# Causal masks of a temporal attention: from mask matmuls to a fused add-and-maximum and a zeroing of the exponentials

## The reference

```python
def _temporal_experts(xt, idx, ...):
    ...
    logits = jnp.einsum('bthd,bshd->bhts', q, k) * HD ** (-0.5)
    causal = jnp.tril(jnp.ones((T, T), dtype=bool))
    logits = jnp.where(causal, logits, -jnp.inf)
    att = jax.nn.softmax(logits, axis=-1)
    o = jnp.einsum('bhts,bshd->bthd', att, v).reshape(B, T, D)
...
xn = _ln(x, norm_s_w, norm_s_b)
spatial_out = _spatial_experts(xn, idx_s, ...)      # attention S, no mask
xt = _ln(x, norm_t_w, norm_t_b)
temporal_out = _temporal_experts(xt, idx_t, ...)    # attention T, causal
fused = _cross_mha(spatial_out, temporal_out, ...)  # attention C, no mask
x = x + fused
```

## The kernel before, in words

| slot | projected, for the next slot | scored | logits from n = 8 | last 8 logits, for n < 8 |
|---|---|---|---|---|
| S slot | T of i | S of i | C of i-2 | T of i-1 |
| T slot | C of i-1 | T of i | S of i | C of i-2 |
| C slot | S of i+1 | C of i-1 | T of i | S of i |

## Time and profile before

### The profile page before, as it was taken

One profiled execution on the slowest core, in us unless ns is written; L12 is line 12 of the kernel. 1 busy time (PEld: TensorE's weight loads), 2 busy tenths in 40 slices (PEclk: granted clock), 3 DMA queues, 4 the chain that ended last, 5 costly groups with the idle time before them and its releaser, 6 DMA issues. The chain is left out here.

```text
span 1797.6 us, 37140 instructions
## 1 busy us (share of the span) xinstructions
PE 1598.6 (89%) x9686; PEld 738.5 (41%) x9686; DVE 1274.2 (71%) x3085; ACT 1217.8 (68%) x2393; POOL 697.2 (39%) x673
## 2 busy tenths in 40 slices
PE   4659946889999999999999999999999999955998
PEld 1217932334444444434444344444444443211665
DVE  5986856388787877878787787878787787352442
ACT  3325741757888878788878878787887878714333
POOL 7822441234344344344334334434434433221442
PEclk9768955989999999999999999999999999857999
DMA  2211125354565455465456456446545635030122
GB/s 51 74 43 37 47 47 71 43 80 60 65 77 66 64 71 79 54 75 74 57 70 77 67 61 79 62 60 76 70 63 69 81 52 65 2 36 26 57 61 59
DMA packets 131811, 108.99 MB, mean 61 GB/s; under 512 B 21809, under 2 KB 124721, under 8 KB 131761
## 3 DMA queue, kind: packets, MB, share of 16 engines
q1 hardware_dynamic: 129712, 104.18, 41.5%
q0 software_dynamic: 2048, 4.20, 0.9%
HBM read 20.05 MB, written 8.39 MB: 16 GB/s over the span
## 5 line engine op out<-in xcount | busy, mean ns | idle before, releaser
L1000 ACT ACTIVATE probs<-psum 128x512 f32<-128x512 f32 (+3 forms) x1536 | 739.6, 551 | 262.4 <-PE psum L1111 159.7
L888 DVE TENSOR_REDUCE mx_S<-psum 128x1 f32<-128x512 f32 x512 | 323.1, 682 | 77.0 <-PE psum L1096 76.5
L888 DVE TENSOR_REDUCE mx_C<-psum 128x1 f32<-128x512 f32 x512 | 319.0, 682 | 56.8 <-PE psum L1096 55.2
L888 DVE TENSOR_REDUCE mx_T<-psum 128x1 f32<-128x128 f32 (+3 forms) x512 | 240.4, 488 | 120.7 <-PE psum L1099 109.5
L824 POOL TENSOR_TENSOR rem_q<-f_q,parts_q 128x512 f32<-128x512 f32 x48 | 55.5, 1155 | 496.9 <-ACT parts_q L986 480.0
L1096 PE MATMUL psum<-ks_S,qs_S 96*128 96x512 bf16 x512 | 201.7, 400 | 26.4 <-DMA ks_S<-parts_k 21.8
L1096 PE MATMUL psum<-ks_C,qs_C 96*128 96x512 bf16 x512 | 202.7, 397 | 12.5 <-DMA ks_C<-parts_k 7.4
L1111 PE MATMUL psum<-qs_C,ks_C 99*128 99x512 bf16 x512 | 194.7, 392 | 18.0 <-ACT probs L1000 10.7
L1111 PE MATMUL psum<-qs_S,ks_S 99*128 99x512 bf16 x512 | 196.0, 384 | 1.6 <-ACT probs L1000 0.9
L1096 PE MATMUL psum<-ks_T,qs_T 96*128 96x128 bf16 (+3 forms) x512 | 157.5, 310 | 7.1 <-DMA ks_T<-parts_k 6.0
L1111 PE MATMUL psum<-qs_T,ks_T 99*128 99x256 bf16 (+3 forms) x512 | 153.3, 302 | 2.5 <-ACT probs L1000 1.7
(11 more groups left out here) (184 smaller groups left out, 2732.5 us busy)
## 6 DMA issues: line engine op xcount, KB each, us to landing
qs_S<-parts_q SPq DMA_DIRECT2D x96, 128.0 KB, 4.5
ks_S<-parts_k SPq DMA_DIRECT2D x96, 128.0 KB, 7.0
qs_T<-parts_q SPq DMA_DIRECT2D x96, 128.0 KB, 4.4
ks_T<-parts_k SPq DMA_DIRECT2D x96, 128.0 KB, 7.0
qs_C<-parts_q SPq DMA_DIRECT2D x96, 128.0 KB, 4.5
ks_C<-parts_k SPq DMA_DIRECT2D x96, 128.0 KB, 6.9
w_in_S<-in_s_in SPq DMA_DIRECT2D x16, 257.0 KB, 2.7
w_in_T<-in_t_in SPq DMA_DIRECT2D x16, 257.0 KB, 2.7
```

The lines of the kernel that those rows point to most:

```text
L888: nc.vector.tensor_reduce(mx[kind][:, n:n + 1], psum[:, ring_place(kind, b, n, RL), 0:last_key], AX_X, ALU.max)\
L1000: nc.scalar.activation(probs[:, n // 4 % 2, n % 4, t0:T], psum[:, LOGITS + ring_place(kind, b, n, RC), t0:T], ACT.Exp, scale=SCALE).then_i ...
```

## The change

- No mask matmul is left, and the tiles `ident_bf`, `mask_row` and `mask_col` go. Scores and logits of T keep their widths; the future half of the diagonal blocks now holds unmasked values.
- `reduce` of T: VectorE's `tensor_tensor_reduce` adds a tile `causal` (128x512, zeros, with -1e30 in the future half of its last 128 columns) to the scores and takes the maximum of the sum in the same instruction; the sum itself is written to a tile `masked`. An increment of a semaphore that nobody waits for (`scored_seen`) stands in front.
- `cut_future`: once the four tiles of a `weigh` are exponentiated, GpSimd's `affine_select` writes zeros into the future half of the four diagonal blocks of `probs2`. `weigh` of T waits for `cut` in place of `exped`.
- GpSimd's sequence is rewritten around the cuts: `split` becomes `remainder` and `low_part`, and the `affine` of `xt` moves from the C slot to the end of the T slot.
- VectorE's start of `attend` waits for `causal`.

```diff
+                def cut_future(kind, b, q):
+
+                    if kind != "T" or not exists(b):
+                        return
+                    pool.wait_ge(exped, TILES * unit_no("T", b) + 4 * q + 4)
+                    pool.sem_inc(cut_seen, 1)
+                    t0 = first_key("T", 4 * q)
+                    diagonal = probs[:, q % 2, :, t0:t0 + P]
+                    nc.gpsimd.affine_select(out=diagonal, in_=diagonal, compare_op=ALU.is_ge, fill=0.0, base=0,
+                                            pattern=[[0, 4], [1, P]], channel_multiplier=-1).then_inc(cut, 1)
...
-                    (kn, bn), _, _, (ko, bo) = units(i, slot)
-                    split(kn, bn)
+                    (kn, bn), _, (kb, bb), (ko, bo) = units(i, slot)
+                    cut_future(ko, bo, 5)
+                    cut_future(ko, bo, 6)
+                    remainder(kn, bn, 0)
+                    cut_future(ko, bo, 7)
+                    remainder(kn, bn, 1)
+                    low_part(kn, bn, 0)
+                    cut_future(kb, bb, 0)
+                    low_part(kn, bn, 1)
                     if exists(bo):
                         u = unit_no(ko, bo)
                         pool.wait_ge(high_out, u + 1)
                         pool.wait_ge(low_out, u + 1)
                         nc.gpsimd.tensor_tensor(s_all[:], s_all[:], s_high[:], ALU.add).then_inc(s_merged, 1)
                         nc.gpsimd.tensor_tensor(u_all[:], u_all[:], u_high[:], ALU.add).then_inc(u_merged, 1)
+                    cut_future(kb, bb, 1)
...
+                    cut_future(kb, bb, 2)
...
                         nc.gpsimd.tensor_tensor(oT[:], u_all[:], s_recip[:], ALU.mult).then_inc(o_ready, 1)
+                    cut_future(kb, bb, 3)
+                    cut_future(kb, bb, 4)
                     if slot == 1 and exists(i + 1):
                         pool.wait_ge(desk_full, desk_use("vS", i) + 1)
                         affine(xn, i + 1, 0, "xn")
-                    if slot == 2 and exists(i + 1):
                         pool.wait_ge(desk_full, desk_use("vT", i) + 1)
                         affine(xt, i + 1, 1, "xt")
...
-                    last_key = P * (n % NB + 1) if kind == "T" else T
-                    nc.vector.tensor_reduce(mx[kind][:, n:n + 1], psum[:, ring_place(kind, b, n, RL), 0:last_key], AX_X, ALU.max)\
-                        .then_inc(reduced, 1)
+                    tile = psum[:, ring_place(kind, b, n, RL), :]
+                    if kind == "T":
+                        dve.sem_inc(scored_seen, 1)
+                        last_key = P * (n % NB + 1)
+                        nc.vector.tensor_tensor_reduce(masked[:, n % RL, 0:last_key], tile[:, 0:last_key],
+                                                       causal[:, T - last_key:T], 1.0, NEG, ALU.add, ALU.max,
+                                                       mx[kind][:, n:n + 1]).then_inc(reduced, 1)
...
-                    pe.wait_ge(exped, TILES * u + 4 * q + 4)
+                    if kind == "T":
+                        pe.wait_ge(cut, 2 * NB * b + q + 1)
+                    else:
+                        pe.wait_ge(exped, TILES * u + 4 * q + 4)
```

More of the change, by code:

```diff
@@ L696, in attend @@
         exped = sem("exped2")
+        cut = sem("cut")
+        cut_seen, scored_seen = sem("cut_seen"), sem("scored_seen")
         summed = sem("summed2")
@@ L814, in affine, with remainder @@
                     nc.gpsimd.tensor_tensor(to[:], scaled[:], s, ALU.add).then_inc(affine_done, 1)
-                def split(kind, b):
+                def remainder(kind, b, c):
                     if not exists(b):
                         return
[L820 to L829, removed]
@@ L831, in slot_program, with low_part @@
-                def slot_program(i, slot):
-                    (kn, bn), _, _, (ko, bo) = units(i, slot)
-                    split(kn, bn)
+                    n = 2 * unit_no(kind, b) + c
+                    pool.wait_ge(hi_done, n + 1)
+                    at_least(pool, mid_done, n - 1)
+                    nc.gpsimd.tensor_tensor(rem[c][:], f32[c][:], parts[c][:, 0, :], ALU.subtract)\
+                        .then_inc(rem_done, 1)
+                def low_part(kind, b, c):
+                    if not exists(b):
+                        return
+                    pool.wait_ge(mid_done, 2 * unit_no(kind, b) + c + 1)
+                    nc.gpsimd.tensor_tensor(parts[c][:, 2, :], rem[c][:], parts[c][:, 1, :], ALU.subtract)\
+                        .then_inc(lo_done, 1)
@@ L862, in _ @@
                 affine(xn, 0, 0, "xn")
-                nc.gpsimd.memset(mask_row[:], 0.0)
-                nc.gpsimd.memset(mask_col[:], 0.0)
+                nc.gpsimd.memset(causal[:], 0.0)
                 for k in KINDS:
@@ L867, in _ @@
                 last.then_inc(ones_in, 1)
-                split("S", 0)
+                for c in range(2):
+                    remainder("S", 0, c)
+                for c in range(2):
+                    low_part("S", 0, c)
                 pool.wait_ge(ones_in, 1)
-                nc.gpsimd.affine_select(out=mask_row[:], in_=mask_row[:], compare_op=ALU.is_ge, fill=NEG, base=0,
-                                        pattern=[[-1, P]], channel_multiplier=1).then_inc(consts, 1)
-                nc.gpsimd.affine_select(out=mask_col[:], in_=mask_col[:], compare_op=ALU.is_ge, fill=NEG, base=0,
-                                        pattern=[[1, P]], channel_multiplier=-1).then_inc(consts, 1)
+                nc.gpsimd.affine_select(out=causal[:, T - P:T], in_=causal[:, T - P:T], compare_op=ALU.is_ge, fill=NEG,
+                                        base=0, pattern=[[-1, P]], channel_multiplier=1).then_inc(consts, 1)
                 affine(xt, 0, 1, "xt")
@@ L963, in _ @@
                 dve.wait_ge(ones_in, 1)
+                dve.wait_ge(consts, 1)
                 values("S", 0)
@@ L1095, in score @@
                     keys = P * (tb + 1) if kind == "T" else T
[L1096 to L1101 removed]
+                    nc.tensor.matmul(psum[:, ring_place(kind, b, n, RL), 0:keys], qs[kind][0:RA, hd, P * tb:P * tb + P],
+                                     ks[kind][0:RA, hd, 0:keys], start=True, stop=True).then_inc(scored, 1)
                 def logits(kind, b, n):
@@ L1110, in logits @@
                     bank = LOGITS + ring_place(kind, b, n, RC)
-                    last = nc.tensor.matmul(psum[:, bank, t0:T], ks[kind][0:RB, hd, P * s:P * s + P],
-                                            qs[kind][0:RB, hd, t0:T], start=True, stop=True)
-                    if kind == "T":
-                        last = nc.tensor.matmul(psum[:, bank, t0:t0 + P], ident_bf[:], mask_col[:],
-                                                start=False, stop=True, skip_group_check=True)
-                    last.then_inc(logits_in, 1)
+                    nc.tensor.matmul(psum[:, bank, t0:T], ks[kind][0:RB, hd, P * s:P * s + P],
+                                     qs[kind][0:RB, hd, t0:T], start=True, stop=True).then_inc(logits_in, 1)
                 def weigh(kind, b, q):
@@ L1184, in _ @@
                 pe.wait_ge(ones_in, 1)
-                pe.wait_ge(consts, 3)
+                pe.wait_ge(consts, 2)
                 pe.wait_ge(w_fixed, 48)
```

15 lines of the change are left out of this document (5 added, 10 removed).

## The result

The changed kernel takes 1858.79 us (median of 4 runs, 1855.93 to 1862.22) against 1797.71 for the kernel before: ratio 1.034, 95% interval 1.0325 to 1.0356. I had forecast 1788.4, and 1812 as the upper end. Its profiled execution has a span of 1854.1 us, 56.5 more than before. One execution of a kernel further down, the one without score masks and with the cut between the merges, took 2515.95 us at a mean clock of 0.56 where its five others took 1788 to 1791; it is left out of that kernel's ratio.

A forecast was written before the change was run, and what follows sets the result against it. TensorE was taken to bound the S and T slots, a DMA landing the C slot. S -0.30, T -0.26, C +0.14 make -0.42 us a round; 14 rounds -5.9, edges -1.5, sum -7.4 from 1795.8: 1788.4 us, range 1780 to 1812.

The forecast's parts named there:

- What bounds the slots: Slot ends: TensorE leads by 0.35 us in S and 0.2 in T, the stacking DMAs by 0.35 in C.
- the chain behind the stall: C slot, from the delayed second `weigh` to the S score: 8.3 to 9.2 us, taken as 8.8; TensorE ready at 830.66.
- The masks, T slot: T slot: slack 0.2 us plus four masks 0.24, minus 0.18 for late `ng`, makes -0.26 (-0.38 to -0.02).
- the good end: T slot: the favourable bound of its range, -0.38 us.
- S slot: S slot: TensorE-bound; five of eight removed masks count, the landing moves with four, giving -0.30 us.
- The fused reduce: VectorE, T slot: two instructions per reduce add 0.12 us a tile (0.06 to 0.24), busy time 18.1 to 22.0.
- the rival in which VectorE takes over the T slot: T slot: VectorE becomes the bound, +1.65 us there, +1.5 per round, 1815 us in all; chance 0.16.
- The cut: GpSimd: each of eight cuts per T unit takes 0.65 us, bounds 0.29 and 1.17.
- Cut 1 and the stall: C slot: cut 1, queued behind `s_all` and `u_all`, holds the second `weigh` to 821.86, a new stall of 2.3 us.
- The clock: Rival: TensorE's granted clock falls, the stall costing 1 us more per round, 1802 us in all; chance 0.04.
- The edges: First and last T unit, run without full slots: -1.5 us of at most 2 x 1.92.
- The bad end of the sum: Unfavourable bounds of the per-round slot terms: +0.48 us a round over 14 rounds, +6.7, 1802.5 us in all.

The follow-up runs named there:

- the cuts alone: Against the kernel before: GpSimd's cuts replace the logit masks, score masks stay on TensorE and VectorE's reduces stay plain; 1812.46 us, ratio 1.0072.
- the two kernels with the cut in the middle: Changed kernel with the second cut moved between GpSimd's two merges, 1806.10 us; the same without score masks and with plain reduces, 1790.27 us.
- the two kernels behind the merges without score masks: Changed kernel without score masks, plain reduces, second cut still after GpSimd's merges, 1814.45 us; the same plus 64 dummy VectorE increments a round, 1857.52 us.
- the padded kernels: Kernel before, all masks kept, with dummy VectorE semaphore increments added per round: 64 took 1821.90 us, 32 took 1798.28, 16 took 1794.73.
- both mended: Changed kernel with second cut between GpSimd's merges and a VectorE loop body as long as before, here by plain reduces without score masks; 1790.27 us.

## Why the prediction was wrong, step by step

- *What bounds the slots.* Right. The C slot with the stall and a full clock was to take 26.91 + 0.14 = 27.05 us; it takes 27.05 with the cuts alone. The chain behind the stall is right too: `weigh` 1 starts there at 911.62, and the S score 8.9 us later, for 8.8 in the forecast. TensorE leads by then, as forecast; its last `weigh` takes 0.99 us and the S score doesn't wait for a DMA:

```profile
919.54 1.07 PE L1156 MATMUL psum<-probs,va_T 128*32 128x512 f32 x8
920.53 0.39 PE L1122 MATMUL psum<-ks_S,qs_S 96*128 96x512 bf16 x1
```

1.7 us of TensorE idle cost 0.2, since the slot's 24 masks (1.44 us) are gone and TensorE had up to 0.35 us to spare before the landing.
- *The masks, T slot.* Forecast -0.26, it was -0.51, outside the -0.38 of the good end: with 0.012 us a pair for 0.12 (below), `ng` isn't late, and the forecast's own sum gives 0.2 + 0.24 + 0.04 = 0.48.
- *S slot.* Forecast -0.30; where nothing is fetched it is -0.11 (26.33, in the cuts alone). Of the 0.48 us of eight masks, 0.17 go into a longer wait for `ng`, as forecast (0.58 for 0.41), and 0.17 into a new wait for VectorE in the ring, which I hadn't counted. The row of the kernel before, then two of the cuts alone:

```profile
832.67 1.12 PE L1079 MATMUL psum<-xt,w_in_T 128*128 128x512 f32 x2 [0.41 <-DVE ng L895]
...
922.68 1.12 PE L1105 MATMUL psum<-xt,w_in_T 128*128 128x512 f32 x2 [0.58 <-DVE ng L920]
...
925.80 0.39 PE L1122 MATMUL psum<-ks_S,qs_S 96*128 96x512 bf16 x1 [0.17 <-DVE mx_S L913]
```

- *The fused reduce.* Forecast +0.12 us a tile. VectorE's busy time in the T slot goes from 18.13 to 18.51: 0.38 / 32 = 0.012. The row of one fused instruction below shows 688 ns for the 686 of the earlier trace rows; the read has 83 ns in its row and hides in the overlap. That also sinks the rival in which VectorE takes over the T slot.
- *The cut.* Forecast 0.65 us, measured 634 ns. *Cut 1 and the stall*: `weigh` 1 forecast 18.25 us into the slot, measured 18.13; of the stall, forecast at 2.3 us, 1.73 are idle, since TensorE comes to it later than forecast.

```profile
L915 DVE CUSTOM_DVE_ANT_0 masked<-psum,causal 128x512 f32<-128x512 f32 x128 | 88.0, 688 | 6.4 <-PE psum L1127 5.1
...
L915 DVE DVE_READ_ACCUMULATOR2_ANT mx_T<- 128x1 f32 x512 | 42.5, 83 | 0.0
...
L843 POOL TENSOR_SCALAR_AFFINE_SELECT probs<-probs 128x512 f32<-128x512 f32 x128 | 80.5, 634 | 203.2 <-ACT probs L1031 203.2
```

- *The clock.* **This step failed.** The sum puts nothing for it, and as a rival it had a chance of 0.04 and a price of 1 us a round: "2 us of stall in 80 is little". It fell in all 13 C slots and cost (53.0 - 13 x 0.2) / 13 = 3.9 us each, 50 us in all. The 80 was the mistake: TensorE's idle share of a round says nothing about 2 us in one piece. By the Trainium skill, TensorE: Matmul & The Clock Gate, Part 1, the gate follows how busy the array has been lately. The runs agree in this: with the stall the clock falls whether the masks' work around it is there (13 of 13 C slots) or not (7 to 13 of 13), and with the cut moved between the merges it doesn't fall in any C slot. They don't make a rule of it: it stayed at 1.00 behind waits of 1.4 to 1.7 us in the changed kernel's S slots.
- *The loop body.* **Missing.** I counted what 64 more instructions a round take to execute (nothing, rightly) and not what it takes to hold them, so that the sum has no term for it: 18 us by the slots, 15.8 between the two kernels with the cut in the middle (1806.1 and 1790.3). Where the stall is there too, the C slots lose 49 us with the longer loop and 31 without it (the two kernels behind the merges without score masks, against 349.0 us in all before). The order of instructions showed the longer loop; I read it for places, not for length.
- *The edges.* Forecast -1.5, measured -8.4 us, and most of it isn't the masks': of 4.3 us ahead of the full slots, 2.4 stand in one S slot (24.77 for 27.21 us, at a clock of 0.76 for 0.69), which takes 24.43 in the kernel with the cuts and all masks; 4.1 stand behind them, where the padded kernels, all masks in place, are also 1.7 to 3.7 us shorter.
- *Slips in the working.* The bad end of the sum is -0.30 - 0.02 + 0.70 = +0.38 a round, not +0.48; the measured time lies far above either. The Trainium skill's page TensorE: Matmul & The Clock Gate does price a mask matmul: its Part 1 gives some 56 ns from start to start for 128 columns, and the 0.06 us of the earlier trace rows agrees.

With both mended, and the score masks dropped instead of moved, the kernel takes 1790.3; 1788.4 was the forecast. That they are so near is in part luck: the T slots and the edges gave more than forecast, the S slots less.

## What to carry to other kernels

Read a new wait of the busiest engine in two parts: what it delays, and what the clock does behind it. In the C slot here 0.5 us in one piece cost nothing, 1 us cost about 1 us more in nearly every slot, and 1.7 us between 0.2 and 4.6. Don't take that for a rule of length: at the S slot's start, waits of 1 us brought a fall in 3 of 12 slots of one kernel and waits of 1.4 to 1.7 us in none of another. Look at the granted clock behind every new wait. A helper engine's step belongs behind what another engine waits for and ahead of what nobody needs yet; one place in a plain sequence decided 53 us here. Before instructions are added to a hardware loop, look at how long the loop is on that engine and at its instruction packets in the DMA view; packets in the middle of the loop are the sign.

## What the runs showed of the hardware

- VectorE held this loop with 32 traced instructions more a round than the 266 before (16 and 32 increments, and the kernel that waits for two tiles), and not with 64 more. With 64, about five packets of 8 KB arrive at each return to the loop's start, and its first reduce of the S slot starts 0.5 to 1.8 us later behind the first score than the 0.42 us of before: least where TensorE waits for a DMA ahead of that score, most where it doesn't.
- The clock's fall comes in two lengths after the same stall, some 3 us and some 10 us, in C slots of 28.0 to 28.3 and 31.3 to 31.5 us; with all masks kept it was always the short one (29.0 us). All 29 long ones began 19.57 to 20.00 us into the slot and no short one did. Why is open.
- A wait of TensorE of 1.06 us was followed by a fall and one of 1.14 us at the same place was not; 12 waits of 1.4 to 1.7 us at the start of the changed kernel's S slots weren't either.
- A fused add-and-maximum from PSUM and SBUF with its accumulator read adds 0.012 us to VectorE's busy time over a plain maximum (18.51 us for 18.13 over 32 tiles).
